# Graph attention with its scores from folded weights, both exponential branches on ScalarE, and the second layer's scores inside its own product

## The reference

```python
h = (x @ W.T).reshape(n, heads, out_ch)
a_src = jnp.einsum('nhc,hc->nh', h, att_src)
a_dst = jnp.einsum('nhc,hc->nh', h, att_dst)
e = jax.nn.leaky_relu(a_src[src] + a_dst[dst], NEG_SLOPE)
m = jax.ops.segment_max(e, dst, num_segments=n)
ex = jnp.exp(e - m[dst])
alpha = ex / (segment_sum(ex, dst)[dst] + EPS)
out = segment_sum(alpha[:, :, None] * h[src], dst)
```

## Time and profile before

| | us |
|---|---|
| median of 3 runs | 1981.26 (1980.11 to 1982.55) |
| profiled execution | 1980.53 |
| its span | 1978.8 |
| TensorE busy | 1826.9 (92%) |
| GpSimd busy | 693.7 (35%) |
| VectorE busy | 921.0 (47%) |
| ScalarE busy | 458.4 (23%) |
| TensorE's share of the chain that ended last | 75% |

### The profile page before, as it was taken

How to read it: one execution, slowest core, us unless ns; L and a number is a source line. 1 busy time by engine, 2 the same in 40 slices (tenths; PEclk the granted TensorE clock), 3 DMA queues, 4 the chain that set the end, 5 groups by cost and what they waited for, 6 DMA issues and landing times.

```text
span 1978.8 us, 27142 instructions
## 1 busy us (share of the span) xinstructions
PE 1826.9 (92%) x10721; PEld 1668.0 (84%) x10721; DVE 921.0 (47%) x2074; ACT 458.4 (23%) x875; POOL 693.7 (35%) x429
## 2 busy tenths in 40 slices
PE   6799999979989876996799999999999999998999
PEld 6699988979978864894477789999999999997899
DVE  8982243245443677845528765111522233225431
ACT  3443132122121214832203231001111011012220
POOL 1028645543345431030200023543534444444454
PEclk9899999989989985897868999999999999999999
DMA  2002212221112110003200001111211111111112
GB/s 79 1 25 73 74 50 63 64 72 42 56 40 86 57 32 16 1 32 79 74 1 10 1 20 47 55 48 47 63 41 56 57 56 56 49 48 49 53 61 71
DMA packets 39761, 94.30 MB, mean 48 GB/s; under 512 B 10306, under 2 KB 11815, under 8 KB 39522
## 3 DMA queue, kind: packets, MB, share of 16 engines
q1 hardware_dynamic: 37828, 87.87, 14.8%
q10 hardware_dynamic: 1822, 4.84, 0.7%
HBM read 90.77 MB, written 1.92 MB: 47 GB/s over the span
## 4 chain that ended last, share of the span: by engine, by line
PE 75%; DVE 10%; issue 3%; ACT 3%; PEld 2%; POOL 1%; PEldq 0%; POOLq 0%; DVEq 0%; ACTq 0%
PE bank L1935 17%; PE bank L1936 16%; PE bank L1937 16%; PE bank L2030 11%; PE bank L2403 6%; PE bank L2310 2%; PEld bank L2164 2%; DVE prob L1641 1%; DVE edge_scores L1555 1%; DVE prob L1646 1%; PE bank L2119 1%; PE bank L2362 1%; PE bank L2220 1%; DVE xT_lo L1859 1%; PE bank L2379 1%
## 5 line engine op out<-in xcount | busy, mean ns | idle before, releaser
L652 POOL TENSOR_TENSOR w_hi<-raw,ones_r 128x768 fp32r<-128x768 f32 (+1 forms) x196 | 300.4, 1533 | 1252.1 <-PE bank L1937 904.7
L655 POOL TENSOR_TENSOR w_lo<-raw,w_hi 128x768 fp32r<-128x768 f32 (+1 forms) x196 | 378.6, 1932 | 15.4
L1935 PE MATMUL bank<-w_hi,xT_hi 128*125 128x384 f32 (+2 forms) x1040 | 357.8, 344 | 12.0 <-POOL w_lo L655 3.9
L1936 PE MATMUL bank<-w_lo,xT_hi 128*125 128x384 f32 (+2 forms) x1040 | 355.3, 342 | 0.0
L1937 PE MATMUL bank<-w_hi,xT_lo 128*125 128x384 f32 (+2 forms) x1040 | 355.1, 341 | 0.0
L1935 PEld LDWEIGHTS bank<-w_hi,xT_hi 128*125 128x125 f32 x1040 | 195.8, 188 | 25.4 <-issue 6.3
L1936 PEld LDWEIGHTS bank<-w_lo,xT_hi 128*125 128x125 f32 x1040 | 195.7, 188 | 5.2
L1937 PEld LDWEIGHTS bank<-w_hi,xT_lo 128*125 128x125 f32 x1040 | 195.5, 188 | 5.1
L1935 PE MATMUL bank<-w_hi,hT_hi 128*125 128x384 f32 x520 | 177.3, 341 | 1.9 <-issue 1.0
L1936 PE MATMUL bank<-w_lo,hT_hi 128*125 128x384 f32 x520 | 176.3, 339 | 0.0
L1937 PE MATMUL bank<-w_hi,hT_lo 128*125 128x384 f32 x520 | 175.9, 338 | 0.0
(11 more groups left out here) (369 smaller groups left out, 2833.0 us busy)
## 6 DMA issues: line engine op xcount, KB each, us to landing
raw<-wa SPq DMA_DIRECT2D x92, 384.0 KB, 3.0
raw<-wc SPq DMA_DIRECT2D x76, 384.0 KB, 3.0
raw<-wb SPq DMA_DIRECT2D x28, 448.0 KB, 3.3
bias<-bias_in ACTq DMA_DIRECT2D x6, 384.0 KB
w_down<-w_down_in SPq DMA_DIRECT2D x8, 288.0 KB, 5.3
w_up<-w_up_in SPq DMA_DIRECT2D x1, 2304.0 KB, 15.4
x<-x_in SPq DMA_DIRECT2D x5, 384.0 KB, 7.9
out<-x SPq DMA_DIRECT2D x10, 168.0 KB
```

What stands on the lines that cost most here:

```text
L652: pool.tensor_tensor(w_hi[:, k, 0:width], raw[:, k, 0:width], ones[:, 0:1].to_broadcast([P, width]), ALU.mult).then_inc(S("unit_high"), 1)
L655: pool.tensor_tensor(w_lo[:, k, 0:width], raw[:, k, 0:width], f(w_hi[:, k, 0:width]), ALU.subtract).then_inc(S("unit_split"), 1)
L1935: pe.matmul(dst, l_hi, r_hi, start=start, stop=False)
L1936: pe.matmul(dst, l_hi, r_lo, start=False, stop=False)
```

## The change

1. **Folded weights.** W1 and W2 are loaded once more, as rows of a head (`w1_in`, `w2_in`). After f0 TensorE multiplies W1's rows with both attention vectors (48 products with 2 columns), the result is split into `folded_1`. For W2 VectorE forms 16 dot products of 768, eight before and eight amid its reads of g1a, in `folded_2`. So the scores come from the layer's input, by `score_rows`, beside g2a and g2b.
2. **One form for rows.** `rows_K` holds high parts in partitions 0 to 63 and low parts in 64 to 127; one fp32r product with `sel` broadcasts a row. `score_columns` turns `rows_K` and sums its blocks. The shifts come in two halves of four heads, 40 rows wide with both parts.
3. **Places inside g2a.** Counted in its 20 jobs (chunk and tile): rows behind jobs 2 and 3, the source broadcasts behind 4 to 17, columns behind 5, the first half of the shifts behind 13, u and v of head 0 behind 15, of head 1 behind 18. From job 15 on ScalarE makes head 0's exponentials. Heads 0 and 1 have `prob` and `uB` buffers of their own.
4. **Two exponentials.** prob = exp(uB[0] + a_src), lesser = exp(uB[1] + a_src/5) on ScalarE; VectorE takes max(min(prob, 3), lesser) and, one tile behind, min(prob, 3) * adj. `lesser` has three buffers.
5. **The loop.** u and v are broadcast two heads ahead, the product follows its head at once, the turn one head behind, mean one head behind, the low part three.
6. **Second layer.** Rows, broadcast, columns, shifts and u, v stand between the steps of g2b; its five banks of a chunk are held, so that the three others serve these groups. The second product runs chunk by chunk.
7. Moved: clearing, `sel` and the reduction of the mask (now before f1's sums), `add_bias("g2")` (now behind the second layer's shifts), the slot weights' transfers (now wait for `g2_h2` and `g2q_prob`).

```diff
+ROWS_AT = {2: 0, 3: 1}
+SOURCES_AT = {4: (0, 1), 7: (2,), 9: (3,), 11: (4,), 13: (5,), 15: (6,), 17: (7,)}
+COLUMNS_AT, SHIFTS_AT, FIRST_SHIFT, NEXT_SHIFT = 5, 13, 15, 18
+LAST_ROWS, LAST_SOURCES, LAST_SHIFTS, LAST_SHIFT = (0, 4), (0, 6), (1, 1), (1, 3)
...
+    def add(label, idx, sem, value, held=False):
+        b = spare.pop(0)
+        if not held:
+            spare.append(b)
+        where[label, idx] = b, user.get(b)
...
-            sp.wait_ge(*E("g2q_uvB_read", 4))
+            sp.wait_ge(*E("g2_h2", 2 * NT))
+            sp.wait_ge(*E("g2q_prob", NT))
...
+            act.wait_ge(*E("f0_low", 24))
+            act.dma_start(w1_first[:], w1_in[0:6].rearrange("h p k -> p h k")).then_inc(S("w1_loaded"), 16)
...
+            act.dma_start(w2_rows[:], w2_in.rearrange("h p k -> p h k")).then_inc(S("w2_loaded"), 16)
...
+            def powers(layer, h, s):
+                made = NT * h + s
+                if s == 0:
+                    act.wait_ge(*E(layer + "_uvB_read", 4 * h + 4))
+                    act.wait_ge(*E(layer + "_fifth", 1))
+                    if h >= 4:
+                        await_group(act, "g2p_agg", 2 * (h - 2) + 1)
+                if made >= 3:
+                    act.wait_ge(*E(layer + "_greater", made - 2))
+                act.activation(prob_of(layer, h)[:, s], uB_of(layer, h)[:, 0], ACT.Exp, bias=a_cols[0:TN, 16 * s + h:16 * s + h + 1])
+                act.activation(lesser[:, made % 3], uB_of(layer, h)[:, 1], ACT.Exp,
+                               bias=a_src5[0:TN, 8 * s + h:8 * s + h + 1]).then_inc(S(layer + "_powers"), 1)
...
+            for h in range(1, HEADS + 3):
+                if h < HEADS:
+                    shifts("g2p", h)
+                    if h == 2:
+                        shift_rows("g2p", 1)
+                    for s in range(NT):
+                        powers("g2p", h, s)
+                if h >= 3:
+                    head_out(h - 3)
...
+            def fold_second(kind):
+                dve.wait_ge(*E("w2_loaded", 32))
+                for k in range(HEADS):
+                    made = kind * HEADS + k
+                    if made >= 2:
+                        dve.wait_ge(*E("second_folded", made - 1))
+                    dve.tensor_tensor_reduce(fold_junk[:, made % 2], w2_rows[:, k], att_2[:, kind], 1.0, 0.0, ALU.mult,
+                                             ALU.add, a_part[:, 2 * k + kind:2 * k + kind + 1]
+                                             ).then_inc(S("second_folded"), 1)
...
+            for h in range(HEADS):
+                greatest_scores("g2p", h)
+                if h == 1:
+                    score_columns("g2p")
+                if h == 3:
+                    shift_parts("g2p", 0, 4)
+            shift_parts("g2p", 1, HEADS)
...
+            def weights_of_edges(layer, h):
+                pr = prob_of(layer, h)
+                for s in range(NT + 1):
+                    made = NT * h + s
+                    if s < NT:
+                        dve.wait_ge(*E(layer + "_powers", made + 1))
+                        STT(pr[:, s], pr[:, s], 3.0, lesser[:, made % 3], ALU.min, ALU.max
+                            ).then_inc(S(layer + "_greater"), 1)
+                    if s:
+                        dve.wait_ge(*E(layer + "_greater", made))
+                        STT(pr[:, s - 1], pr[:, s - 1], 3.0, f(adj[:, s - 1]), ALU.min, ALU.mult
+                            ).then_inc(S(layer + "_prob"), 1)
...
+            for h in range(HEADS + 3):
+                if h < HEADS:
+                    weights_of_edges("g2p", h)
+                if 1 <= h <= HEADS:
+                    head_mean(h - 1)
+                if h >= 3:
+                    head_low(h - 3)
...
+            def score_rows(layer, c, folded, hi, lo, k):
+                c0, cn = CH[c]
+                dst = open_bank(layer + "_rows", c)
+                for j in range(k):
+                    pe.matmul(dst[0:64, 0:cn], folded[:, j], hi[:, j, c0:c0 + cn], start=j == 0, stop=False)
+                    last = pe.matmul(dst[0:64, 0:cn], folded[:, j], lo[:, j, c0:c0 + cn], start=False, stop=j == k - 1)
+                close(last, layer + "_rows", c)
...
+            for h in range(HEADS + 1):
+                if h + 2 < HEADS:
+                    shift_broadcast("g2p", h + 2)
+                if h < HEADS:
+                    head_product(h)
+                if h == 0:
+                    shift_rows("g2p", 1)
+                if h:
+                    turn_head(h - 1)
...
+            down("g2b", "g2b", hT_hi, hT_lo, lambda k: pe.wait_ge(*E("g2p_low", k + 1)), beside=last_scores)
+            pe.wait_ge(*E("g2_h2", NT))
```

More of the change, by code:

```diff
@@ L165, in several, with several_from @@
             add(label, i, sem, first + (i + 1) * per)
+    def several_from(label, first, n, sem):
+        for i in range(first, first + n):
+            add(label, i, sem, i + 1)
     def sweep(label, before_last=()):
@@ L191, in ffn, with pairs @@
             several(f + "_down", 2 * NT, f + "_x")
[L193 to L208, removed]
+    def pairs(label, first=0, n=2):
+        for i in range(first, first + n):
+            add(label, i, label + "_read", i + 1)
     sweep("A", (("g0_maxT", 0, "g0_max_read", 1), ("g0_maxB", 0, "g0_maxB_read", 1)))
@@ L470, in network @@
         sel8 = sm(SLOTS)
[L471 removed]
+        a_cols, a_src5, a_max = sm(NT * 16), sm(NT * 8), sm(NT * 8)
         no_edge, slot_sum, unoffset = sm(NT), sm(KD * 4), sm(1)
@@ L958, in _ @@
+            for c in range(2):
+                rows_high("g2q", c)
+            source_rows("g2q", 0)
+            second_rows(0)
+            shift_rows("g2q", 0)
+            shifts("g2q", 0)
+            for s in range(NT):
+                powers("g2q", 0, s)
+            second_rows(1)
             act.wait_ge(*E("slots_squared", 1))
@@ L1975, in up, with down @@
                     pe.drain().then_inc(S("unit_used"), 1)
-            def down(key, label, lhs_hi, lhs_lo, ready, feed=0, seed=None, after=None, tile_ready=None, turn=None):
+            def down(key, label, lhs_hi, lhs_lo, ready, feed=0, seed=None, after=None, tile_ready=None, turn=None,
+                     beside=None):
                 kt, cw, chunks, per = DOWN[key]
@@ L2013, in down @@
                             turn(n - TURN_LAG)
+                        if beside and n == NT - 1:
+                            beside(c, k)
                     if after:
@@ L2180, in _ @@
             expert_layer("f0", 12, 0)
+            pe.wait_ge(*E("w1_loaded", 32))
+            dst = open_bank("g2_fold", 0)
+            for h in range(HEADS):
+                weights = w1_first[:, h] if h < 6 else w1_last[:, h - 6]
+                for k in range(KD):
+                    last = pe.matmul(dst[:, 0:16 * KD].rearrange("p (k t e) -> p k e t", k=KD, t=2)[:, k, h],
+                                     weights[:, k * P:(k + 1) * P], col("att1").rearrange("p (t e) -> p e t", t=2)[:, h],
+                                     start=True, stop=True)
+            close(last, "g2_fold", 0)
             pe.wait_ge(*E("self_loops", NT))
@@ L2255, in attention, with shift_rows @@
-            def attention(layer, heads, product):
-                pe.wait_ge(*E(layer + "_uv", 2))
-                for i in range(4):
-                    a, b = ((0, 4), (4, NT))[i % 2]
+                        last = pe.transpose(dst[0:TN, (n - a) * P:(n - a + 1) * P], f(rows_K[:, n * TN:(n + 1) * TN]),
+                                            ident[:])
+                    close(last, layer + "_colT", i)
+            def shift_rows(layer, half):
+                pe.wait_ge(*E(layer + "_uv", half + 1))
+                for i, (a, b) in ((2 * half, (0, 4)), (2 * half + 1, (4, NT))):
```

606 lines of the change are left out of this document (311 added, 295 removed).

## The result

The changed kernel takes 1933.34 us (median of 4 runs, 1930.6 to 1940.08), the kernel before 1981.9 us on the same chip (4 runs, 1980.11 to 1982.64). The ratio is 0.9761, with a 95% interval of 0.9735 to 0.9788. The forecast was 1930, in a range of 1915 to 1950. The profiled execution took 1934.34 us, with a span of 1932.6.

A forecast was written before the change was run, and what follows sets the result against it. TensorE, busy 92% of the span, bounds the kernel; only its waits and low-clock stretches can give much. 1980.5 - 35 - 4 - 0 - 13 - 1.7 + 3 = 1929.8, so 1930 us; 8 in 10 between 1915 and 1950.

The forecast's parts named there:

- Step 1: Up to the first weight: 773.4 becomes 738, VectorE's maxima, slowed beside GpSimd's splits, setting the pace; gain 35 us.
- step 6: Folding in the first two layers: a loss of 3 us (0 to 7; 10 if second-layer loads are late too).
- The first weight after 745: Sign of being wrong, for the stretch up to the first weight, which was forecast near 738.
- Step 2: Head loop: 80.3 us become 76, ScalarE the full engine at 10.1 us a round; bounds 72 and 98.
- Rival A: Head loop keeps its old round of 12.3 us: 98 us instead of 76, time 1952; 15%.
- E: VectorE stays the bound; moving scores into g2a frees only the 17 us of dot products; time 1949; 5%.
- B: VectorE and GpSimd meet seldom (first weight at 727), g2b has no bank wait (51 us): time 1915; 15%.
- Rival D: Slower than before: head loop's pairs run one after the other, 19 us a head, time 2006; 3%.
- Step 3: Last weight to g2b's start: unchanged at 7 us.
- Step 4: g2b to the second product: 67.9 us become 55, with a 4 us bank wait; gain 13; bounds 51 and 67.
- Step 5: Second product, 34.67 us before: gain 1.7 us, with no pause before it.
- Rival C: Folding on the path, 10 us more than forecast, through late weights or starved unit loads: time 1940; 12%.

The follow-up runs named there:

- narrow splits: Changed kernel with GpSimd's two instructions of each g2a unit handling 8 columns in place of 768 (stale weights): 1922.86 us, ratio 0.9701.
- handed splits: Changed kernel with six weight units' splits during g2a handed from GpSimd to ScalarE (high half) and VectorE (low half): 1931.41 us, ratio 0.9753.
- the kernel with all three: Changed kernel with six splits handed to ScalarE and VectorE, fold of heads 6 and 7 before f1's router, second eight dot products moved: 1927.12 us.
- lock step: Changed kernel with ScalarE waiting, before each pair of exponentials, for VectorE's larger-of-two on the pair before: 1964.41 us, ratio 0.9921.
- the last kernel: The kernel with all three, with GpSimd's split of the two units behind them waiting for the first layer's last weight: 1917.4 us, ratio 0.9696.

## Why the prediction came out right, step by step

**Step 1 (35 forecast, 35.9 measured).** Right in mechanism and size, counted from the turned rows. The maxima began 17.2 us after the turned rows (17.1 forecast), and the first weight came 53.0 us after them (53.4). Four bursts appeared with pitches of 2.0 and 2.4 us. That the exclusion was on the path was read from the earlier trace rows alone; the kernels with narrow and with handed splits show it (from the first maximum to the first weight 8.5 us less, 6.4 less, and 11.8 less with the last burst gone too). By the rule of the Trainium skill cited there (SBUF — State Buffer, section "Who interferes with whom"), the trace agrees: maxima of 2.06 and 2.44 us beside splits of 2.04 and 2.29, 0.80 free. The floor without exclusion was forecast at 718 to 727; with narrow splits the first weight is at 736.1, of which 10.8 us are step 6's, so 725; without the burst that this kernel still meets at its end it would be near 720 (an estimate from the 5.4 us that such a burst cost in the kernel with all three). What no run shows is how the 35.9 us divide between the dot products that are gone, the scores' place beside g2a and the early exponentials of heads 0 and 1: step 1's placing was never undone, so that division stays argued from the rows.

Two of the prediction's own signs need a word. "The first weight after 745" was named as a sign of being wrong, and it came at 748.3 and 747.5; the maxima were to begin at about 684 and began at 695.3. Both marks are late by what stands ahead of g2a: the turned rows came at 678.1, and the prediction's 738 was counted from 667.4. So it is step 6's loss that these signs show, not a fault in step 1.

**Step 2 (76 forecast, 72.6 measured).** ScalarE rules, with rounds of 10.07 us (10.1 forecast); two kernels show it from both sides. The 3.5 us put on for imperfect overlap was not needed. Rival A (rounds of 12.3) is out, and so is E, which gave step 1 a gain of 17 us. B is out as well: bursts met the maxima and g2b had its bank wait. Rival D's mechanism, which this kernel does not have, shows when it is forced: under a lock step the round is 14.03 us, not 19, because ScalarE's next pair overlaps VectorE's second instruction; even so the kernel would have stayed 0.8% faster than before (1964).

**Step 3 (7 forecast, 7.1 measured).** As said.

**Step 4 (55 forecast, 52.6 measured).** One bank wait inside g2b, as said, but of 1.7 us instead of 4: only one of the five maxima met a split, where two were assumed. Undone, the placing costs 10 to 12 us.

**Step 5 (1.7 forecast, 2.1 measured).** As said; the product starts 0.37 us after g2b.

**Step 6 (a loss of 3 forecast, 10.8 measured).** This is the term that was mis-sized, and it hid behind the other errors. I had read "x96" of the earlier trace rows, 15.50 us for 96, as 96 products, 0.16 each. That loop has 8 experts by 6 tiles, 48 products: the trace records each product of two plain f32 operands as two instructions (48 as 96 there and in the fold, and 6 as 12 when the fold was cut). The price per product was 0.32 at half clock, and 48 of them are 15.5 us, not 7.7; measured 16.0. That these two agree so closely is partly luck: the fold's 128-wide weights cost 0.44 per product at half clock (12 in 5.3 us), and its first 36 products ran mostly faster (0.30 each). Against 10.5 us of idle TensorE (from 431.3 to 441.8) that leaves 5.5 us on the path, and 6.0 is what came back when the fold was cut. The dot products' part was right: 3.5 us measured at the gather's end when they were moved, 3 forecast. 6.0 and 3.5 are 9.5 of the 10.8 us; the last 1.3 us are open. The fold starts 0.9 us later than the gather did before, but that mark moves as much from one execution to the next (429.9 to 431.9), and g2a's first result moves by several. Rival C put the fold on the path with 10 us more than forecast, and 8 came; but its mechanism, late weights or starved units, did not: the fold's products wait for no load.

**The sum.** Errors of -0.9, -3.4, -2.4 and -0.4 in steps 1, 2, 4 and 5 stand against +7.8 in step 6 and 3 to 4 from the lower clock late in that execution. Together they make the 4.5 us by which the profiled execution is above the sum (1934.3 against 1929.8). That the point came so close is luck: terms of up to 8 us cancelled.

## What to carry to other kernels

Check the count of a group against its loop before dividing: the trace's instructions are not the source's products where operands are plain f32. Work put into an engine's gap costs only what sticks out of the gap, so the price must be right exactly there. And when a chain on VectorE of two-operand instructions is the bound, a gain of the size seen here (11.8 us from the first maximum to the first weight) can lie in taking GpSimd's work from beside it: to ScalarE, or to a moment at which VectorE waits anyway. And before a mark of a trace is compared with another trace's, look at where the two stand ahead of the edit: here code that was the same differed by up to 7 us.

## What the runs showed of the hardware that I had not expected

- VectorE instructions of 20 columns took 1.65, 1.39 and 1.67 us beside a split, 0.18 alone. The loss does not shrink with the instruction: three short ones lost 4.2 us here, where a maximum loses 1.3 to 1.6. The Trainium skill (SBUF — State Buffer, section "Who interferes with whom") says that a VectorE instruction with two SBUF inputs contends with a GpSimd instruction that reads SBUF, for a port pair that is locked exclusively; the trace agrees, in that each slow one ends 0.03 us after the GpSimd instruction beside it.
- ScalarE's copies of 128 x 768 (836 ns each) ran beside the maxima and cost them nothing (805 ns in the mean). The same section of the Trainium skill says that ScalarE waits on nobody; the trace agrees, as in the last kernel the two copies ahead of the first maximum and the four amid the maxima take the same 1.57 us a pair.
- With TensorE at work in all but small gaps, the same instructions ran mostly at the higher clock in one execution and at half in the next: the first 72 fold instructions have a median of 251 or 252 ns in most runs, and 353 in two (the fold then ends near 450.3 instead of 447.3 to 448.6; the granted clock between 430 and 445 us was 0.60 in one of these, 0.71 in the changed kernel). Gains of 3 us in front of such a stretch cannot be told from this spread by the time of a few runs.
